# A static four-engine attention pipeline: the pieces of a unit in a new order

## The reference

```python
q, k, v = (short_conv(x @ w, conv_w) for ...)          # 4 taps, then silu
k_unit = k / (norm(k) + EPS)
v_hat = k @ proxy_w;  err = v - v_hat
feats = stack([entropy, norm(err)/norm(v), cos(v, v_hat), log1p(norm(err))]) ++ head_embed
hf = silu(silu(feats @ mlp_w1 + b1) @ mlp_w2 + b2)
beta_fast, beta_slow, lam, amp_fast, amp_slow = sigmoids of hf @ small weights
decay = exp(g_chan * amp)                               # per channel and token
def step(S, ...):                                       # delta rule, over 512 tokens
    Sd = S * decay
    S_new = Sd + outer(k * beta, v - k @ Sd)
    return S_new, q @ S_new
o = lam * o_fast + (1 - lam) * o_slow
o = o / rms(o) * onorm_w * sigmoid(x @ g1 @ g2 + b);  out = o @ wo
```

## Time and profile before

| | us |
|---|---|
| median of 3 runs | 4295.09 |
| lowest, highest | 4289.88, 4296.61 |
| profiled execution, own time | 4301.73 |
| its span, first to last instruction | 4299.9 |
| TensorE busy in the span | 4000.7 (93%) |
| VectorE, ScalarE, GpSimd busy | 3105.3, 2296.8, 933.6 |
| mean granted TensorE clock | 0.96 |

### The profile page before, as it was taken

How to read it: one execution, slowest core, us unless ns; L and a number is a source line. 1 busy time by engine, 2 the same in 40 slices (tenths; PEclk the granted TensorE clock), 3 DMA queues, 4 the chain that set the end, 5 groups by cost and what they waited for, 6 DMA issues and landing times. The chain is left out here.

```text
span 4299.9 us, 179869 instructions
## 1 busy us (share of the span) xinstructions
PE 4000.7 (93%) x76866; PEld 2486.6 (58%) x76866; DVE 3105.3 (72%) x5135; ACT 2296.8 (53%) x6321; POOL 933.6 (22%) x1927
## 2 busy tenths in 40 slices
PE   7999999999999999999999999757879789999998
PEld 4667767767676676767667676522333334444443
DVE  4788888888888888888888887478999991212221
ACT  4577776676676667676676766444344331111110
POOL 1333333333333333333233333100000000000000
PEclk8999999999999999999999999778989899999999
DMA  2222222222221212212122221142323332000000
GB/s 76 65 60 71 65 69 68 58 76 66 63 68 59 77 52 75 70 56 78 57 70 70 63 71 49 41 148 72 94 83 96 92 121 89 29 1 30 0 20 10
DMA packets 133721, 277.31 MB, mean 64 GB/s; under 512 B 21004, under 2 KB 62496, under 8 KB 129472
## 3 DMA queue, kind: packets, MB, share of 16 engines
q1 hardware_dynamic: 132784, 265.60, 20.2%
q10 hardware_dynamic: 144, 0.20, 0.0%
HBM read 235.07 MB, written 30.67 MB: 62 GB/s over the span
## 5 line engine op out<-in xcount | busy, mean ns | idle before, releaser
L420 PE MATMUL a_pb<-a_x_t,a_w_qkv 128*128 128x512 f32 x1536 | 844.0, 641 | 15.5 <-DMA a_x_t<-in_x_t 8.2
L1318 DVE TENSOR_TENSOR a_nq<-a_nq,a_tot 128x1024 f32<-128x1024 f32 x320 | 392.8, 1227 | 133.9 <-PE a_pb L451 85.2
L1281 DVE SCALAR_TENSOR_TENSOR a_acc<-a_pb,a_taps,a_acc 128x511 f32<-128x511 f32 (+2 forms) x576 | 425.5, 739 | 31.1 <-ACT a_acc L866 17.4
L2119 PE MATMUL m_p_y<-m_h,k_ident_sb 128*128 128x512 f32 x512 | 285.4, 710 | 130.7 <-DVE m_h L2356 130.7
L2830 DVE TENSOR_TENSOR a_x_t<-f_gate,f_pb 128x512 f32<-128x512 f32 x128 | 88.0, 687 | 383.1 <-ACT f_gate L2754 383.1
L2754 ACT ACTIVATE f_gate<-f_pb 128x512 f32<-128x512 f32 x132 | 78.8, 597 | 411.7 <-PE f_pb L2695 275.4
L420 PEld LDWEIGHTS a_pb<-a_x_t,a_w_qkv 128*128 128x128 f32 x1536 | 241.1, 192 | 99.0 <-issue 67.4
L451 PEld LDWEIGHTS a_pb<-a_nq,a_ks 128*32 128x32 f32 x20480 | 214.3, 111 | 143.3 <-issue 112.8
L2350 DVE TENSOR_TENSOR_SCAN m_h<-m_da,m_h 128x2048 f32<-128x2048 f32 x64 | 283.1, 4424 | 17.7 <-ACT m_da L2262 12.4
L1718 POOL COPY a_apt<-a_apt_fine 32x256 f32<-32x256 f32 x256 | 100.5, 393 | 882.4 <-DVE a_apt_fine L1336 857.8
L2119 PEld LDWEIGHTS m_p_y<-m_h,k_ident_sb 128*128 128x128 f32 x512 | 112.7, 228 | 295.1 <-DVE m_h L2356 161.9
(11 more groups left out here) (332 smaller groups left out, 8841.6 us busy)
## 6 DMA issues: line engine op xcount, KB each, us to landing
a_rows<-rows SPq DMA_DIRECT2D x192, 512.0 KB, 3.9
a_amp_sums<-amp_sums SPq DMA_DIRECT2D x64, 508.0 KB, 3.7
attn_o<-a_o_out SPq DMA_DIRECT2D x64, 256.0 KB, 2.7
m_b_rows<-ssm_bc SPq DMA_DIRECT2D x64, 256.0 KB, 3.7
m_c_rows<-ssm_bc SPq DMA_DIRECT2D x64, 256.0 KB, 4.5
k_big<-attn_o SPq DMA_DIRECT2D x16, 1024.0 KB, 8.3
a_w_qkv<-in_w_qkv SPq DMA_DIRECT2D x48, 256.0 KB, 3.2
k_big<-in_w_gu SPq DMA_DIRECT2D x3, 1536.0 KB, 13.3
```

The lines of the kernel that those rows point to most:

```text
L420: mm = nc.tensor.matmul(pb[:, V_BANK if i == P_V else KQ_BANK], w_qkv[:, i, k], x_t[:, k, b * T:(b + 1) * T], start=(k == 0), stop=(k == D ...
L1281: last = nc.vector.scalar_tensor_tensor(acc[:, i, d:T], src[:, 0:T - d], taps[:, i, 3 - d:4 - d], acc[:, i, d:T], ALU.mult, ALU.add)
L1318: last = nc.vector.tensor_tensor(part, part, spread(blocks, list(part.shape)), ALU.mult)
L2119: nc.tensor.matmul(p_y[:, et], ident[:], h[:, (b * DS + n) % 3, et], start=(n == 0), stop=(n == DS - 1), skip_group_check=True).then_inc(s ...
```

## The change

The same pieces with the same waits, semaphores and buffers are listed in another order on TensorE, ScalarE, VectorE and GpSimd. SyncE's order stays. The slot number runs from -4 to UNITS+4, where it ran from -3 to UNITS+3, since some pieces now stand a slot further back (`later = s.at(-2)` is new). The pieces that occur only at the start or the end (`unsure`, `gate_low`, `keep_g`, `ssm_first`, `entropy` and the like) sit in other slots; the steps of `ssm_first` were spread over slots UNITS-1 to UNITS+2 and are now over UNITS-1 to UNITS+4.

The core of the diff: the range, and GpSimd's list entire.

```diff
-    for n in range(-3, UNITS + 4):
+    for n in range(-4, UNITS + 5):
...
                 def slot(s):
                     late = s.at(-1)
+                    later = s.at(-2)
+                    if later.has(0):
+                        spread_y(later)
+                    if later.has(1):
+                        reset_y(later)
                     if late.has(1):
                         gates_vals(late)
-                    if late.has(0):
-                        spread_apt(late)
                     if late.has(-2):
                         root_o(late)
+                    if late.has(0):
+                        spread_apt(late)
                     if late.has(2):
                         norms_dens(late)
-                    if late.has(0):
-                        spread_y(late)
                     if late.has(2):
                         make_feats(late)
-                    if late.has(1):
-                        reset_y(late)
```

More of the change, by code:

```diff
@@ L769, in slot @@
[L769 to L782, removed]
@@ L1124, in slot @@
                     late = s.at(-1)
+                    later = s.at(-2)
+                    if later.has(0):
+                        copy_w(later, 4)
+                    if later.has(-1):
+                        copy_o(later, 2)
+                    if later.has(0):
+                        copy_32(later)
+                    if s.n == UNITS + 2:
+                        ssm_first(FIRST_U)
+                    if s.n == 1:
+                        log_sum(2)
+                    if later.has(1):
+                        exp_tot(later)
@@ new lines, in slot @@
+                    if later.has(1):
+                        exp_e1(later)
+                    if later.has(0):
+                        copy_64(later)
+                    if later.has(-1):
+                        copy_u(later, 3)
+                    if s.n == UNITS + 4:
+                        ssm_first(FIRST_LN)
+                    if late.has(-1):
+                        scale_r0(late)
+                    if later.has(0):
+                        copy_w(later, 5)
+                    if s.n == 1:
+                        keep_g(2)
@@ new lines, in slot @@
+                    if late.has(-1):
+                        copy_kt(late, 0)
+                    if s.n == UNITS + 2:
+                        ssm_first(FIRST_DBL)
+                    if later.has(2):
+                        log_err(later)
+                    if later.has(3):
+                        tap(later, 3, P_V)
+                    if later.has(-1):
+                        copy_o(later, 3)
+                    if s.n == UNITS + 1:
+                        ssm_first(1)
+                    if later.has(0):
+                        copy_xy32(later)
@@ new lines, in slot @@
+                    if later.has(2):
+                        copy_feats(later)
+                    if later.has(0):
+                        copy_w(later, 6)
+                    if late.has(1):
+                        hide_1(late)
+                    if s.n == -1:
+                        log_sum(1)
+                    if s.n == UNITS + 3:
+                        ssm_first(FIRST_DT + 2)
+                    if later.has(0):
+                        copy_y64(later)
+                    if late.has(1):
+                        hide_2(late)
@@ L1173, in slot @@
                     if late.has(-1):
-                        copy_kt(late, 2)
+                        copy_u(late, 1)
+                    if s.n == -3:
+                        widen(1)
+                    if late.has(-3):
+                        tanh_gate(late)
+                    if late.has(2):
+                        silu(late, 2, P_Q)
+                    if s.n == UNITS + 3:
+                        ssm_first(FIRST_EXP)
+                    if late.has(-1):
+                        copy_o(late, 1)
@@ new lines, in slot @@
+                    if later.has(1):
+                        prepare_nq(later, QUERY)
+                    if late.has(2):
+                        convolve(late, 2, P_V, 1)
+                    if s.n == -3:
+                        lower(1)
+                    if s.n == 1:
+                        entropy(2)
+                    if late.has(2):
+                        convolve(late, 2, P_V, 2)
+                    if s.n == UNITS + 1:
+                        ssm_first(1)
+                    if late.has(0):
+                        decay_nq(late, 0)
```

479 lines of the change are left out of this document (210 added, 269 removed).

## The result

The changed kernel takes 4911.65 us (median of 4 runs, 4908.35 to 4933.74) against 4295.85 us of the kernel before: a ratio of 1.145, 95% interval 1.142 to 1.148. It is 616 us slower where 117 were forecast, far above the top of the range. The profiled execution has a span of 4912.8 us and a mean granted TensorE clock of 0.894, where before it was 0.96.

What follows compares the result with a forecast made beforehand. TensorE, busy 2354 of 2400 us, was taken as the bound. Floor 37.9, W64 wait 3.2 and fetch 2.2 made 43.3 us per unit against 41.4, +117 us over 61 units: 4412 us, range 4300 to 4495.

Steps and rivals of the forecast that it cites:

- The floor: TensorE's unit without any stall: 40.0 us before, 37.9 after 2.1 us saved; the other 1.35 us before was stall.
- mode changes: TensorE switching between full and tiled matmuls: fewer switches save 1.7 us per unit, fewer drains 0.4.
- The queue ahead of `spread_y`: On GpSimd, make_feats now waits for log_err ahead of spread_y, so TensorE stands 3.2 us at W64 each unit.
- The rival of a faster kernel: ScalarE reaches log_err within 5.9 us of W4, no wait at W64: 39.2 us per unit, 4165 us; chance 0.18.
- Fetch: Dense tiled runs on TensorE outrun instruction blocks of 256: 2.2 us of stall per unit outside W4 to W64.
- fetch hidden: Rival: W64 wait real, dense tiled stretches cost almost nothing in fetch: 41.7 us per unit, about 4315 us; chance 0.18.
- Others: ScalarE tables, GpSimd's norms_dens, VectorE, SyncE and the slots at both ends: taken as 0, ends within -10 to +10 us.
- Period: 37.9 + 3.2 + 2.2 = 43.3 us: Unit period as floor plus W64 wait plus fetch stalls, against 41.4 before: +1.9 us, times 61 is +117 us.
- Both slower cases: W64 wait with fetch stalls, 4412 us, chance 0.57; W64 wait with fetch hidden, around 4315 us, chance 0.18.

Runs made afterwards that it cites:

- e2: The kernel before with one move on GpSimd, make_feats ahead of spread_y, all other orders old: 4762.24 us.
- e12: The kernel before with the matmuls of P1 to P4 issued twice, the same sums again: 4752.28 us.
- e13: The kernel before with the first K chunk's full matmuls issued four times, the same sum: 4445.69 us.
- e14: e2 with TensorE's Q0 moved behind XY32 and issued seven times, filling the wait with useless work: 4592.3 us, ratio 1.072.
- e4: The changed kernel with TensorE's project pieces Q1 to Q3 pulled ahead of the wait at W64: 4689.2 us.
- e5: The changed kernel with make_feats behind spread_y, FEATS behind W64 and Q1, HID1 behind Y64, and copy_w(6) ahead of copy_feats: 4560.02 us, ratio 1.066.
- e10: e5 with TensorE's ROWS moved behind ev1 and turn_v: 4619.54 us, ratio 1.078.
- e1: The changed kernel with GpSimd's make_feats put back behind spread_y: 4725.35 us, ratio 1.105.

## Why the prediction was wrong

*The floor.* "Floor of a unit: 37.9 us." The changed kernel's rest is 38.0. The level held partly by luck. The prediction took 40.0 from one clean unit and called all of the 1.35 above it stall, but the earlier trace rows itself leaves TensorE idle only 45.5 us in 58 units, 0.8 each, and the rest before is 40.5. So the floor began 0.5 too low, and the saving is 2.5 where 2.1 were written; the counts and prices of the mode changes come out near, and the two misses cancel.

*The queue ahead of `spread_y`.* Right in mechanism, place and size: 14.4 us from W4 to W64 forecast, 15.8 in the unit shown and in the median of the stretch; TensorE stands 3.6 us in each unit where 3.2 were written. e2 shows that the GpSimd order alone makes such a wait. The rival of a faster kernel needed `log_err` to be early; it was not.

*Fetch.* 2.2 us per unit were taken outside W4 to W64, with bounds 1 and 3.6. Measured are 2.5 inside tiled runs, 2.3 of them outside W4 to W64, and some 0.4 at the starts of runs, in the bounds. e12 and e13 show the mechanism. By the Trainium skill ("Runtime: NRT & Kernel Launch", "Instruction fetch mechanics") the cost of crossing into the next block is mostly hidden; the trace does not agree for tiled matmuls, with 2.5 us per unit of stalls inside their runs, and the rival "fetch hidden" needed it to.

*ROWS.* "Others" had nothing for it, and ROWS waits 0.7 us per unit for GpSimd's `gates_vals`: a term at zero that should have had a price. The chain heads, ScalarE's tanh, `gates_vals` is not later than before: the tanh starts 1.1 us behind heads, before 1.4, and ROWS 5.4 us behind heads in both kernels (medians). But before, seven pieces of TensorE filled these 5.4 us without a wait (turn_v ev1 X1 proxy gate P3 u1), and now only five stand there (u0 Q3 od0 W1 P2).

*The step that failed* is the sum "Period: 37.9 + 3.2 + 2.2 = 43.3 us". It prices a microsecond of waiting at a microsecond. The sum has no term for the clock: the earlier trace rows shows it at 1.00 in a stretch where TensorE is busy 98%, and the forecast took that as given for the new order. The half rate cost 5.7 us per unit, 5.6 more than before, or some 340 of the 616 us, beside 6.7 us of added idle time. 3.9 of the 5.7 lie behind falls that have the W64 wait as their longest stand-still, the others behind ROWS and the stalls inside runs. The written sum with this term and the true waits: 38.0 + 7.5 + 5.7 = 51.2. That a stand-still at W64 brings the clock down is shown by e2 and e14, in the orders of the kernel before: there the same wait with work in it leaves the clock alone. In the changed order it is not the whole cause, since e4 takes the W64 wait away and still loses 5.0.

*The rivals.* Slower was forecast with 0.75, but no case had this size. Both slower cases were bounded by waits alone, so the range ended at 4495.

The result splits, per unit: -2.5 for mode changes; +3.6 wait at W64; +0.7 at ROWS; +1.9 more stalls inside tiled runs; +0.5 other idle time; +5.6 half rate. That is +9.8, against 9.85 measured.

What stays open: what exactly of the engine's doing brings the clock down when no wait is long, as in e4. There it fell behind stretches of tiled and short pieces with waits of up to half a microsecond between them; whether the tiled work or the waits did it was not separated. The idle time alone does not tell it: e4 stands still 4.7 us per unit and loses 5.0 at the half rate, e5 stands still 5.2 and loses 1.8, e12 4.4 and 1.0.

## What to carry to other kernels

A static order that keeps one engine 98% busy may rest on that engine's full clock; price a new wait on it at its length and at the slower work behind it (here 5.5 us of wait cost 3.0 more in e2, and 3.6 us cost 3.9 more in the changed kernel). Filling a wait with pieces taken from later in the list can lose the clock there instead (e4). Before pieces are reordered for cheaper mode changes, write down for each piece what its old neighbours hid (a copy's latency, the fetch of the next instructions), since both come back as waits. When a piece that waits for another engine is put ahead of one that others need, follow that engine's whole list up to the awaited piece, however idle the queue's own engine is.

## What the runs showed of the hardware

- During or right behind each stand-still of TensorE at W64, of 3.6 us on average in the changed kernel (47) and 5.5 in e2 (49), the granted clock fell to the 1.2 GHz level, for 8.4 and 8.1 us on average; with the wait filled by matmuls of 512 columns, no microsecond of 2400 was at that level (e14). In e4 the clock fell 49 times with no stand-still above 0.53 us in the 10 us ahead.
- The blocks of 256 TensorE instructions never started closer than 3.2 us in the stretch (before, changed, e12), and most stalls inside tiled runs ended 2.3 to 2.8 us behind a block's start. Doubling four tiled pieces (512 instructions, 2.7 us of array time) cost 7.1 us per unit (e12), while 2.6 us of full matmuls cost 2.6 (e13).
- A wait on a semaphore ahead of a tiled run can be free: with ROWS moved, 1.0 us of it went and 1.3 us of stalls inside tiled runs came (e10).
- GpSimd's small instructions took different times in different orders. The same multiply of 128x4 (L1742, L1745 after) had a mean of 0.27 us in the kernel before, 0.20 in the changed one and 0.83 in e1; what makes the difference was not tried.
